# Spatial gate logits on all partitions, tanh gates and another order of a mixer's tail

## What is computed

```python
out = conv2d(x, w1, b1) + conv2d(x, w3, b3, pad=1) + conv2d(x, w5, b5, pad=2)
avg, mx = mean(out, (2, 3)), max(out, (2, 3))
ca  = sigmoid(ca_mlp(avg) + ca_mlp(mx))              # one gate for each channel
c   = out * ca
sa_in = concatenate([mean(c, 1), max(c, 1)], 1)      # two features of each pixel
sa  = sigmoid(conv2d(sa_in, sa_w, pad=3))            # 7x7: one gate for each pixel
cbam_out = c * sa
...                                                  # q, k, v by 1x1 convolutions
attn = softmax(exp(-dist_sq(q, k) / (2 * sigma**2)))
non_local = out + (attn @ v)
return conv2d(concatenate([cbam_out, non_local], 1), tail_w, tail_b)
```

## Time and profile before

| what | us |
|---|---|
| median of 3 runs | 209.7 |
| lowest and highest | 209.54, 209.79 |
| profiled execution | 208.21 |
| its span | 206.40 |
| PE busy in it | 195.5 (95%) |
| DVE, ACT, POOL busy | 126.8, 127.7, 42.5 |
| granted TensorE clock | 1.0 of full speed |

### The profile page before, as it was taken

How to read it: one execution, slowest core, us unless ns; L and a number is a source line. 1 busy time by engine, 2 the same in 40 slices (tenths; PEclk the granted TensorE clock), 3 DMA queues, 4 the chain that set the end, 5 groups by cost and what they waited for, 6 DMA issues and landing times.

```text
span 206.4 us, 3091 instructions
## 1 busy us (share of the span) xinstructions
PE 195.5 (95%) x1120; PEld 91.2 (44%) x1120; DVE 126.8 (61%) x367; ACT 127.7 (62%) x213; POOL 42.5 (21%) x60
## 2 busy tenths in 40 slices
PE   7998999999999998999999999999999998699995
PEld 3654222348876764322222354533224496242222
DVE  0467879957641824954436348496475688677555
ACT  2626688646345683866667550498676684588763
POOL 7743000000000000102974000020750022020570
DMA  6999400000000000000000000000000000000001
GB/s 214 353 412 406 156 2 0 0 0 3 2 3 0 3 0 0 0 5 0 0 0 0 0 0 3 0 0 0 0 6 2 0 0 3 0 0 0 0 0 54
DMA packets 3119, 8.40 MB, mean 41 GB/s; under 512 B 550, under 2 KB 1072, under 8 KB 2976
## 3 DMA queue, kind: packets, MB, share of 16 engines
q1 hardware_dynamic: 2736, 7.60, 9.8%
q0 software_dynamic: 224, 0.46, 0.7%
q10 hardware_dynamic: 144, 0.13, 0.3%
HBM read 7.94 MB, written 0.26 MB: 40 GB/s over the span
## 4 chain that ended last, share of the span: by engine, by line
PE 79%; DVE 11%; ACT 7%; issue 2%; DVEq 0%; ACTq 0%
PE bank L367 18%; PE banks L384 9%; PE banks L295 8%; PE banks L385 7%; PE banks L560 6%; PE bank L306 4%; PE bank L300 4%; ACT hidden L732 3%; PE bank L348 3%; PE banks L521 2%; PE banks L502 2%; PE bank L617 2%; PE bank L485 2%; PE bank L329 2%; ACT rstd L694 1%
## 5 line engine op out<-in xcount | busy, mean ns | idle before, releaser
L732 ACT ACTIVATE hidden<-banks,pack_l 128x1024 f32<-128x1024 f32 (+1 forms) x43 | 44.9, 1053 | 19.5 <-PE banks L385 19.0
L367 PE MATMUL bank<-hidden,w 128*64 128x512 f32 (+1 forms) x160 | 41.4, 596 | 1.3 <-ACT hidden L732 1.3
L295 PE MATMUL banks<-idle_work 128*128 128x512 bf16 x123 | 31.7, 392 | 1.2 <-DVE idle_work L1015 1.2
L384 PE MATMUL banks<-split_x,w_hi 128*128 128x512 f16 x80 | 30.7, 384 | 0.0
L385 PE MATMUL banks<-split_x,w_lo 128*128 128x512 f16 x80 | 30.3, 379 | 0.0
L1457 POOL CAST split_x<-normed 64x256 f16<-64x256 f32 x8 | 3.9, 495 | 97.5 <-DVE normed L901 95.2
L384 PEld LDWEIGHTS banks<-split_x,w_hi 128*128 128x128 f16 x80 | 7.7, 97 | 27.2 <-issue 12.0
L690 ACT ACTIVATE squares<-bank 128x256 f32<-128x256 f32 x18 | 6.9, 383 | 20.8 <-PE bank L300 20.6
L295 PEld LDWEIGHTS banks<-idle_work 128*128 128x128 bf16 x123 | 12.2, 104 | 15.8 <-issue 4.4
L1466 POOL TENSOR_TENSOR total<-total,term 128x512 f32<-128x512 f32 x12 | 17.6, 1465 | 2.6 <-DVE term L992 2.0
L367 PEld LDWEIGHTS bank<-hidden,w 128*64 128x64 f32 x160 | 7.9, 134 | 18.7 <-issue 13.6
(11 more groups left out here) (316 smaller groups left out, 321.1 us busy)
## 6 DMA issues: line engine op xcount, KB each, us to landing
w_stage<-in_w SPq DMA_DIRECT2D x3, 512.0 KB, 13.8
w_stage<-in_w SPq DMA_DIRECT2D x1, 1024.0 KB, 11.1
conv<-in_conv SPq DMA_DIRECT2D x1, 800.0 KB, 8.2
w<-in_w SPq DMA_DIRECT2D x3, 256.0 KB, 14.0
w<-in_w SPq DMA_DIRECT2D x1, 512.0 KB, 11.1
toeplitz<-in_toeplitz SPq DMA_DIRECT2D x1, 512.0 KB, 11.7
gauss<-in_gauss SPq DMA_DIRECT2D x1, 512.0 KB, 12.9
pack_l<-in_pack_l SPq DMA_DIRECT2D x1, 373.5 KB, 14.9
```

What stands on the lines that cost most here:

```text
L295: mm(out, idle_work[:, 0:128], idle_work[:, 0:cols], start=True, stop=True)
L367: last = mm(out[64 * h:64 * h + 64, cut], w2[l][:, (f * NE + e) * CH:(f * NE + e + 1) * CH], hidden[v % 3][:, h * 512 + cut.start:h * 512 ...
L384: mm(out, w1_hi[l][:, at:at + 128], split_x[h][:, :], start=True, stop=False)
L732: last = act(hidden[u % 3][:, cut], both[u % 2][:, cut], ACT.Gelu, bias=P(f"l{l}", "e_b1")[:, e * fc + f:e * fc + f + 1])
```

## The change

Five things are changed.

1. `spatial_gates` uses one feature column repeated 64 times as the stationary operand, once for each half, so that the logits of a half come out on all of its 64 partitions: eight matmuls with 64 columns in place of four with two. `spatial_map`, `to_half`, its DMA and `gate_logits` are dropped.
2. Both gates are taken as tanh of half the logit, straight from PSUM on ScalarE. The channel gate is 0.5 * tanh + 0.5; the spatial one is 1 + tanh, and its factor 0.5 is multiplied into the weight `tail0` once, on POOL. Clamps, reciprocal, exp and ln are dropped. The table set loaded before layer 1's and layer 3's exponentials is `exp_and_others` in place of `natural_log_exp_and_others`.
3. `attend(0)` is issued in three pieces: the third row stands where `spatial_map(0)` stood.
4. `gate_both(1)` stands before `normalise(1)` on VectorE, and `tail(1)` takes the gated part first, as `tail(0)` does.
5. `average(4, 0)` stands between `tail(1)` and `center(4, 1)`.

```diff
             def spatial_gates(j):
...
                 for c in range(2):
                     for n in range(2):
-                        at = 8 * j + 4 * c + 2 * n
-                        last = mm(gate_ps[j][0:2, 0:PIX], sa_feat[:, at:at + 2],
-                                  toeplitz[:, (2 * c + n) * PIX:(2 * c + n + 1) * PIX],
-                                  start=c + n == 0, stop=c + n == 2)
+                        for h in range(HALVES):
+                            at = 8 * j + 4 * c + 2 * n + h
+                            last = mm(gate_ps[j][64 * h:64 * h + 64, 0:PIX], sa_feat[:, at:at + 1].broadcast_to([128, CH]),
+                                      toeplitz[:, (2 * c + n) * PIX:(2 * c + n + 1) * PIX],
+                                      start=c + n == 0, stop=c + n == 2)
...
-            def spatial_map(j):
-
-                pe.wait_ge(S["sa_map"], j + 1)
-                mm(gate_ps[j][:, 0:PIX], to_half[:, :], sa[:, 4 * PIX * j + 3 * PIX:4 * PIX * (j + 1)],
-                   start=True, stop=True).then_inc(S["sa_bc"], 1)
...
-                for n, (weight, ready, src) in enumerate(pairs if j == 0 else pairs[::-1]):
+                for n, (weight, ready, src) in enumerate(pairs):
...
             channel_hidden(1)
-            spatial_map(0)
+            attend(0, range(2, 3))
             channel_gates(1)
-            attend(0, range(2, 4))
+            attend(0, range(3, 4))
...
-            spatial_map(1)
             tail(1)
+            average(4, 0)
             center(4, 1, x[3], x_ready(3))
-            averages(4)
+            average(4, 1)
+            busy(NORM_TAIL[4], bank[0][:, :])
...
             def gate_pixels(j):
 
-                part = [sa[:, (4 * j + n) * PIX:(4 * j + n + 1) * PIX] for n in range(4)]
-                sc.wait_ge(S["sa_cl"], j + 1)
-                st.link(act(part[1], part[0], ACT.Exp, scale=-1.0))
-                st.link(act(part[2], part[1], ACT.Ln, bias=P("first", "one")[0:2, :]))
-                act(part[3], part[2], ACT.Exp, scale=-1.0).then_inc(S["sa_map"], 1)
+                sc.wait_ge(S["sa_ps"], j + 1)
+                tanh_half(chunk(sa, j), gate_ps[j][:, 0:PIX]).then_inc(S["sa_map"], 1)
...
-                        sc.wait_ge(S["ca_cl"], j + 1)
-                        act(ca[:, 4 * j + 1:4 * j + 2], ca[:, 4 * j:4 * j + 1], ACT.Exp, scale=-1.0)\
-                            .then_inc(S["ca_e"], 1)
+                        sc.wait_ge(S["ca_s"], j + 1)
+                        tanh_half(ca[:, 2 * j:2 * j + 1], gate_ps[j][:, 0:1]).then_inc(S["ca_e"], 1)
...
-                    if h == 0:
-                        ve.wait_ge(S["ca_s"], j + 1)
-                        TS(gate[0], gate_ps[j][:, 0:1], -80.0, None, ALU.max).then_inc(S["ca_cl"], 1)
                 ve.wait_ge(S["ca_e"], j + 1)
-                st.link(TS(gate[2], gate[1], 1.0, None, ALU.add))
-                st.link(V.reciprocal(gate[3], gate[2]))
-                TS(chunk(gated, j), chunk(O, j), gate[3], None, ALU.mult).then_inc(S["gated_c"], 1)
+                st.link(TS(gate, tanh, 0.5, 0.5, ALU.mult, ALU.add))
+                TS(chunk(gated, j), chunk(O, j), gate, None, ALU.mult).then_inc(S["gated_c"], 1)
...
             def gate_both(j):
-                ve.wait_ge(S["sa_bc"], j + 1)
-                TT(chunk(cbam, j), gate_ps[j][:, 0:PIX], chunk(gated, j), ALU.mult).then_inc(S["cbam_done"], 1)
+
+                ve.wait_ge(S["sa_map"], j + 1)
+                STT(chunk(cbam, j), chunk(sa, j), 1.0, chunk(gated, j), ALU.add, ALU.mult).then_inc(S["cbam_done"], 1)
...
             normalise(0)
-            gate_logits(1)
             add_input(0)
+            gate_both(1)
             normalise(1)
-            gate_both(1)
             add_input(1)
...
+            setup.link(G.tensor_scalar(P("l1", "tail0"), P("l1", "tail0"), 0.5, None, ALU.mult))
```

More of the change, by code:

```diff
@@ L85, in metaformer @@
         ca2 = sb("ca2", [8, 128])
-        to_half = sb("to_half", [2, 128])
         select = sb("select", [48, EXPERTS * 128], BF16)
@@ L115, in metaformer @@
         names = """act_chain ao_ps att_exp att_in att_ps attn bn_ab bn_out bn_ps bn_rstd bn_stats bn_var
-            borders_zero c_tok ca_cl ca_e ca_h ca_in ca_r ca_s ca_top cbam_done conv_done conv_loaded
+            borders_zero c_tok ca_e ca_h ca_in ca_r ca_s ca_top cbam_done conv_done conv_loaded
             conv_out conv_split corner_w ctx_ps ctx_sb dist dve_chain e_key e_lev field_bias final_ps
@@ L123, in metaformer @@
             q_max q_ps q_sb qc_ps qc_sb qk_done qk_lin qk_sb qk_sq route_exp route_logits route_logits0
-            route_parts routed route_rows route_shift route_transposed sa_bc sa_cl sa_in sa_map sa_ps small_loaded
+            route_parts routed route_rows route_shift route_transposed sa_in sa_map sa_ps small_loaded
             split_hi0 split_hi1 split_lo tail toeplitz_loaded tok_a tok_d tok_ps v3_ps v3_rows
@@ L191, in metaformer @@
         ca = sb("ca", [128, 4 * INNER])
-        sa = sb("sa", [2, 4 * COLS])
+        sa = sb("sa", [128, COLS])
         sa_feat = sb("sa_feat", [128, 16])
@@ L220, in metaformer @@
         bias_out = sb("bias_out", [128, 1])
-        SETUP = 8
-        ROOTS, LOGS = "abs_reciprocal_sqrt_and_small", "natural_log_exp_and_others"
+        SETUP = 9
+        ROOTS, EXPS = "abs_reciprocal_sqrt_and_small", "exp_and_others"
         NE = EXPERTS
@@ L462, in channel_gates @@
             def channel_gates(j):
-                pe.wait_ge(S["small_loaded"], 64)
+                pe.wait_ge(S["small_loaded"], 48)
                 pe.wait_ge(S["ca_r"], j + 1)
@@ L794, in _ @@
                         grid(chunk(normed[3], j)[64 * h:64 * h + 64, :]), ACT.Copy).then_inc(S["v_hi"], 1)
-            nc.scalar.preload_act_table_set(LOGS)
+            nc.scalar.preload_act_table_set(EXPS)
             sc.wait_ge(S["pool_setup"], SETUP)
@@ L1151, in gate_channels @@
                 mean, top = stats[:, 2 * j:2 * j + 1], stats[:, 2 * j + 1:2 * j + 2]
-                gate = [ca[:, 4 * j + n:4 * j + n + 1] for n in range(4)]
+                tanh, gate = ca[:, 2 * j:2 * j + 1], ca[:, 2 * j + 1:2 * j + 2]
                 ve.wait_ge(S["conv_out"], j + 1)
@@ L1214, in _ @@
             token_features(0)
-            gate_logits(0)
             gate_channels(1)
@@ L1399, in _ @@
             po.dma_start(ca2[:, :], a["ca2"]).then_inc(S["small_loaded"], 16)
-            po.dma_start(to_half[:, :], a["to_half"]).then_inc(S["small_loaded"], 16)
             setup = Steps(po, "pool_setup")
@@ L1593 @@
     arrays["ca2"] = _both_halves(v["L1_conv_ca_w2"][:, :, 0, 0].T)
-    arrays["to_half"] = np.repeat(np.eye(2, dtype=np.float32), 64, axis=1)
     sel = np.zeros((2, 3, 8, 8, 2, 64), np.float32)
```

## The result

The changed kernel took 208.31 us (median of 4 runs, 208.22 to 208.68) against 209.75 (4 runs, 209.54 to 210.10): ratio 0.993, 95% interval 0.9912 to 0.9948. The first comparison gives a gain of 1.44 us where 0.88 was forecast.

A forecast was written before the change was run, and what follows sets the result against it. PE's chain was taken to bound layer 1's mixer up to 77.06 us, hand-overs after it. Gains 0.58 + 0.26 + 0.04 = 0.88 us, taken off the median 209.7, gave about 208.85 us; range 208.3 to 209.9.

The forecast's parts named there:

- What bounds the kernel: Layer 1's mixer: PE's chain without a gap up to 77.06 us, then a row of hand-overs between VectorE and PE.
- Part 1: Last hand-over of layer 1's mixer: with gate_both(1) and the gated part first, the tail waits last for normalise(1); gain 0.58 us.
- The cover: VectorE before gate_both(1): free near 76.0 us, a full microsecond before attend(1) ends, so the gate's new place costs nothing.
- Part 2: spatial_map(0) leaves PE; VectorE's gated product limits the gain to 0.26 us, not 0.62; spatial_map(1) leaving counts 0.
- Part 3: Gates' matmuls, both images: a pair on alternating halves costs as much as one matmul; net gain 0.04 us.
- the sum: Whole kernel: 0.58 + 0.26 + 0.04 = 0.88 us off, giving about 208.85 us.
- Part 4: Averages, POOL's extra step, clamps and exp/ln on ScalarE, and the table load: all counted at nothing.
- Dear pairs: Gates' matmuls: a pair costs 0.51 to 0.54 us whatever its neighbours; time 209.3 to 209.55, no change; chance 0.2.
- loads in the open: Gates' matmuls, both images: 64-column f32 loads are not hidden, making the kernel slower, 210.7 us; chance 0.12.
- the late gate: sa_map(1) comes after 77 us, so gate_both(1) delays normalise(1); 0.58 shrinks to some 0.15, time 209.3; chance 0.02.
- more than that: PE's early arrival brings up to 0.38 us and fewer half-to-full-width changes 0.1 to 0.2 more: 208.4 to 208.6; chance 0.06.

The follow-up runs named there:

- the delayed kernel: Changed kernel plus five idle matmuls (1.07 us) between the two images' convolutions in layer 1: mean 209.72 us over 12 runs, ratio 0.9994 to the kernel before.
- the variants' traces: Traces of changed-kernel variants, each with a further edit; two that lost clock took 105.68 to 105.71 us from add_input(1) to layer 3's router logits.
- filled kernels: Ten idle matmuls added in layer 3's mixer: kernel before, mean 208.76 us; changed kernel, 207.95; three later versions of the changed kernel keep them.

## Why the prediction was right or wrong, point by point

- **What bounds the kernel.** Right in the main. PE's chain up to attend(1) and hand-overs behind it; both could be lengthened and shortened where the rows said. But the hand-overs don't begin at 77.06: the chain of before runs on PE, through spatial_map(1), to 78.31.
- **Part 1, 0.58.** 0.57 measured (1.36 to 0.79). The size was right, its account not quite: 0.15 of it is the price of spatial_map(1), which part 2 put at zero because PE "would wait anyway". PE did wait, but gate_both(1) waited for that matmul. A removed step on an engine that idles still counts if somebody waits for its result. The cover held: gate_both(1) ran from 76.46 to 76.87, ahead of the end of attend(1) at 78.11.
- **Part 2, 0.26.** Right. gated_tokens(1) starts 22.10 us after the convolution's start before and 21.62 after. Of these 0.48, 0.22 are won by the start of attend(0) (18.04 and 17.82 us after the convolution's start), by image 0's gates and the matmuls behind them; the rest, 0.26, is the product. But PE stood there for 0.14 us, not 0.35: from the step behind channel_hidden(1) to values(1) it is 1.97 us before (67.35 to 69.32) and 1.56 after (68.58 to 70.14), 0.41 less where a piece of 0.62 had left. The split of attend(0) thus costs PE some 0.2, which that wait hid.
- **Part 3, +0.04.** Right in both images: 0.09 less and 0.06 more. Weight loads of 0.134 us hide beside the matmuls of the other half, for a repeated column too, and the rule of the Trainium skill (page "TensorE: Matmul & The Clock Gate", Part 3: loads overlap only when the row group differs) doesn't hold here, where both halves have one row group. What I left out is that the convolution goes on at once behind gates on half the columns: its next 32 records take 1.83 us, and before they took 1.95, as this row of the chain before says. Most of the 0.11 by which the sum fell short is that.

```profile
63.94 1.95 PE banks L560 x32
```

- **Part 4 and the sum, the step that failed.** "Nothing later is changed, so the rest moves along", and with it the step that takes the 1.5 us between the profiled execution and the median off as a constant, and the sentence that the clock should stay at 1.00. In the two traces first compared the clock does stay. In two of three executions of before it doesn't: some 1.05 us are lost in layer 3, 100 us behind the change. Moving that stretch forward took the loss from 64 of 97 runs to 5 of 16, worth (0.66 - 0.31) x 1.05 = 0.37 on average, and the delayed kernel took it back. The mean of all these runs is 209.63 before and 208.33 after, 1.30 apart, where 0.99 + 0.37 makes 1.36. I read the clock in the one profiled execution, which was free of it and had the earliest start of all traces, and even noted that this execution was 1.5 us below the median, but asked only for its difference and not for its cause. Both causes were the clock's, a late rise at the start (read from the matmuls' times) and the fall in layer 3 (on record).
- **What was luck.** The 1.44 us of the first comparison are not explained by a rarer fall: three of its four changed runs had it. Their times, 208.22 to 208.39, less 1.05 are those of the earliest starts. None of the four runs of before was under 209.54, where 18 of the later 97 were; whether they had the half clock is not on record. So the 1.44 is 0.99 from the mixer and 0.45 from which starts and clocks four runs on each side happened to get.
- **Rivals.** Dear pairs, loads in the open and the late gate did not come; "more than that" named the right side by the wrong mechanism.

What stays open: the size of the second effect. 5 of 16 against 64 of 97 is a wide estimate, and since the fall spares early and late starts of before alike, a change that brings the stretch forward by another amount may make it more frequent. No unfilled trace of the changed kernel itself caught the fall; that it lies in layer 3 there rests on the variants' traces and on its absence once the stretch was filled.

## What to carry to other kernels

Compare two traces by the stretch between two fixed events, since 0.01 us can be read there while the runs spread over 2 us. When one profiled execution differs from the median by more than the change is worth, find out why before summing: here a gain of 0.99 came out as 1.33 over 12 runs, in part because a shift of 1 us changed which runs lost clock in a thinly filled stretch, and as 1.44 over 4 by chance on top. Fill such a stretch with idle matmuls on both sides of a comparison (0.9 us in the means of before here; 13 of 20 runs times 1.05 makes 0.7, the rest is the start's spread), and order matmuls on half the columns so that neighbours use different halves.

## What the hardware showed that I had not expected

- The granted clock fell to 0.50 for 3.4 us, in 64 of 97 executions of before, behind a stretch in which PE was busy 2.2 to 2.9 of 4 us in the traces with and without the fall. With 3.75 to 3.87 of 4 busy (five filled kernels) it fell in none of 41. The fall costs 1.05 us.
- At the program's start the same 11 matmuls of 512 columns take 3.92 to 4.88 us, and the convolution starts 1.45 us apart with it; with eight instead of eleven the times of the filled kernel spread by 1.0 us instead of 1.46.
- Eight f32 matmuls on 64 columns cost 1.73 us with the halves alternating and 2.58 with them in turn. Between full-width neighbours the alternating ones cost 1.88.
- A stationary operand that repeats one column loads about as fast as another of 64 columns: 132/137/138 ns (min, median, max) against 132/134/136 for L452.

```profile
L502 PEld LDWEIGHTS banks<-toeplitz,sa_feat x32: 132/137/138, 63.3 to 74.4; 128*64 128x64 f32 x32
```
